# New hand-laid orders, PSUM banks and two VectorE forms in a four-stage transformer kernel

## The chip, the cores and the metric

The program runs on one core of one Trainium2 chip. The metric is the device time of one execution in microseconds (us); lower is better. TensorE is PE in the rows (PEld its weight loads), VectorE DVE, ScalarE ACT, GpSimd POOL, SyncE SP.

## The reference

x has 8 batches of 256 tokens by 128 features, float32. Four residual stages follow each other, each on a layer norm of x:

```
x = x + attn_a(layernorm(x))      # Q, K, V by sigmoid projections; A from |mean Q - mean K|, no softmax; (A @ V) @ Wo + bo
x = x + ffn(layernorm(x))         # w_down(silu(w_gate x) * (w_up x)), 384 hidden, int weights / 127
x = x + attn_b(layernorm(x))      # 16 heads of 64, causal softmax, + biases
x = x + ffn(layernorm(x))         # the same ffn again
```

In attn_a, with t = 1 - mean over features of Q (and of K), delta = t_Q - t_K transposed, f = 0.9 exp(-|delta| / 0.5), and A = f + 0.9 where delta < 0, else -f + 0.9.

## The kernel before

The kernel keeps x in SBUF as 16 tiles of 128 tokens by 128 features, two tiles (256 tokens) to a batch b. The work is cut into small **jobs** with a name and a number; each engine runs its own list of jobs, written out as a string (`ORDER`), so that all 8 batches overlap as a pipeline. Semaphores alone tie the lists together. The letter at the end of a name tells the stage: A is the first attention, F the first ffn, B the softmax attention, P the second ffn.

Jobs of one batch b: lnsA (VectorE makes the statistics at lines 695 to 702, `var` among them; GpSimd makes rstd by a power at line 855 and the normalised xn at line 866, batch 0 has xn on VectorE at line 712), lntA (TensorE transposes xn; ScalarE copies it rounded as xt_hi, line 571, VectorE makes the rest xt_lo, line 768), qkv0 to qkv2 (three f32r matmuls each), mean (means of Q and K; VectorE makes tq, ntk and the 0/1 tile `less`, lines 726 to 732), dist (ScalarE: |delta| and exp), sign (VectorE, `signed`, line 787), stdp (GpSimd), sv, vwo, aout (TensorE; VectorE adds to x, line 743). The ffn: lnsF, lntF, gF0 to gF2 (gate and up matmuls; ScalarE tanh; two VectorE instructions, lines 779 and 780, make the hidden tile), dbF (TensorE, line 430; VectorE adds to x, line 747). The softmax attention: lnsB, lntB (rt_hi, rt_lo), v0 to v3, and for each of the 64 head pairs m: qk.m (six f32r matmuls; VectorE adds the bias, line 824), scores.m (eight short f32 matmuls, two banks s0 and s1), mask.m (VectorE, lines 797 and 799: minus the masked score and its maximum), exp.m (ScalarE), inverse.m (VectorE), norm.m (GpSimd, line 908), transposes.m (TensorE, banks t0 and t1; evacuated by ScalarE and VectorE), and for two pairs together sum.m (line 536). out0 and out1 multiply by Wo and VectorE adds to x (line 754); the last batch has part of them done ahead as pre0, pre1. The second ffn is lnsP, lntP, gP, dbP, and SyncE stores a batch when dbP has been added.

Four more kinds: w0 to w5 split the big weights into wqkv_hi (ScalarE) and wqkv_lo (GpSimd, line 888); bv copies a bias out on VectorE (line 757); bo is a matmul for the output bias (line 442), computed once; hot is filler for TensorE, four transposes of the identity whose result nobody reads.

Matmuls of qkv, g, v and qk have f32r operands; all others have f32 operands, and for each the profile shows two matmuls where the program has one (transposes one). TensorE writes into eight PSUM banks. `BANKS` gives for each job the bank of its n-th instance, one digit each. A bank is taken again only when its reader has released it: `take` waits for that. Rings of buffers limit the head pairs: three for qk, two for neg_s, four for prob.

```
ORDER = {"PE": "lntA.0 hot.0 hot.1 qkv1.0 ...", "ACT": ..., "DVE": ..., "POOL": ...}
def take(job, n):
    if turns[job, n] > 1:
        pe.wait_ge(g_free[bank_of(job, n)], turns[job, n] - 1)
```

In the rows below, L350 to L352 are the f32r matmuls of qkv, v and qk, L368 transposes of lnt, L410 and L411 the ffn's gate and up, L430 db, L449 to L451 the filler, L457 pre, L464 out, L536 sum.

Of the kernel before, what the change touches and what calls it, by code (L numbers as in the profile page):

```python
# [21 lines left out]
P = 128  # L22
# [31 lines left out]
        sum.3 transposes.4 transposes.5 qk.9 aout.2 v2.0 v2.1 scores.8 scores.9 transposes.6 transposes.7 sum.5 qk.10 lntF.2
        v1.1 v3.1 qk.11 gF0.2 scores.10 transposes.8 scores.11 transposes.9 sum.7 lntA.3 gF2.2 gF1.2 qk.12 qk.13 out0.0 qkv0.3
        qkv2.3 dbF.2 scores.12 scores.13 sum.9 transposes.10 transposes.11 qk.14 qk.15 qkv1.3 out1.0 lntB.2 mean.3 transposes.12
        scores.14 sum.11 scores.15 transposes.13 qk.16 lntP.0 vwo.3 qk.17 aout.3 gP0.0 v1.2 v2.2 gP2.0 sum.13 transposes.14
        transposes.15 scores.16 scores.17 v3.2 lntF.3 qk.18 v0.2 qk.19 gF2.3 gF1.3 gF0.3 sum.15 scores.18 transposes.16
        scores.19 transposes.17 gP1.0 out0.1 dbF.3 lntA.4 qk.20 qk.21 sum.17 scores.20 scores.21 transposes.18 transposes.19
        qkv1.4 lntB.3 out1.1 qkv2.4 qkv0.4 qk.22 qk.23 mean.4 scores.22 scores.23 sum.19 transposes.20 transposes.21 qk.24  # L60
        lntP.1 dbP.0 gP0.1 vwo.4 v0.3 qk.25 aout.4 gP2.1 scores.24 scores.25 sum.21 transposes.22 transposes.23 lntF.4 qk.26
        qk.27 v2.3 v1.3 gF0.4 sum.23 scores.26 scores.27 transposes.24 transposes.25 gF2.4 qk.28 gF1.4 lntA.5 qk.29 out0.2 dbF.4
        sum.25 scores.28 transposes.26 transposes.27 scores.29 qkv1.5 gP1.1 out1.2 qkv0.5 qk.30 qk.31 lntB.4 v3.3 mean.5 qkv2.5
        transposes.28 scores.30 scores.31 transposes.29 sum.27 v0.4 dbP.1 lntP.2 vwo.5 qk.32 qk.33 aout.5 gP2.2 scores.32 sum.29
        transposes.30 transposes.31 scores.33 qk.34 lntF.5 v1.4 qk.35 gP0.2 v2.4 gF0.5 transposes.32 scores.34 scores.35 sum.31
        transposes.33 qk.36 gF1.5 lntA.6 gF2.5 out0.3 qk.37 qk.38 dbF.5 qkv1.6 qkv0.6 scores.36 scores.37 transposes.34
# [884 lines left out]
```

## Time and profile before

| | |
|---|---|
| median of 3 runs | 340.31 us (340.23 to 340.88) |
| the profiled execution: its own time | 340.77 us |
| its span, first to last instruction | 338.7 us |
| TensorE busy | 319.7 us (94%) |
| VectorE / ScalarE / GpSimd busy | 269.0 / 231.5 / 198.5 us |
| DMA | 5.83 MB; nearly all in the first 20 us |

The time of an execution is its span and about 2 us around it. A share of busy time is a mean over stages. Matmuls are pipelined, so two of them overlap in the rows and the distance from start to start tells their cost better than their length. An engine's instructions run in the order of its list, so one that is late holds all behind it.

### The profile page before, as it was taken

How to read it: one execution, taken by the hardware profiler on the slowest of the kernel's cores; microseconds unless marked ns; L12 is line 12 of the kernel's file. 1: busy time of each engine (PE TensorE's matmuls, PEld its weight loads, DVE VectorE, ACT ScalarE, POOL GpSimd, SP SyncE). 2: the span in 40 equal slices, each digit the busy share in tenths (PEclk: the TensorE clock that was granted, in tenths of full speed). 3: DMA queues.
4: the chain of work that ended last, by engine and by line, in shares of the span. 5: the costliest groups of instructions: out<-in, count | busy, mean ns of one | idle time of the engine just before them, and what ended most of it. 6: DMA issues, size and time to landing. Idle time of an engine off the chain costs nothing. (4 is left out here: it accounts for less than half of the span.)

```text
span 338.7 us, 9997 instructions
## 1 busy us (share of the span) xinstructions
PE 319.7 (94%) x3264; PEld 278.0 (82%) x3264; DVE 269.0 (79%) x1092; ACT 231.5 (68%) x784; POOL 198.5 (59%) x265
## 2 busy tenths in 40 slices
PE   2888999999999998999999999999999999999995
PEld 2767788889888977889988888889988878888875
DVE  4468799988987889878979879878787897967645
ACT  2643678876688858576887757777868738787811
POOL 4585456778745657947566197742757186355600
PEclk9999999999999999999999999999999999999999
DMA  7900000000000000000000000000000000000001
GB/s 194 296 0 3 1 2 4 2 1 3 2 2 2 2 2 3 15 3 3 2 16 4 2 2 1 18 2 0 4 17 0 3 3 17 3 0 3 3 15 33
DMA packets 6418, 5.83 MB, mean 17 GB/s; under 512 B 864, under 2 KB 5856, under 8 KB 6368
## 3 DMA queue, kind: packets, MB, share of 16 engines
q1 hardware_dynamic: 6080, 4.99, 5.0%
...
HBM read 4.15 MB, written 1.05 MB: 15 GB/s over the span
## 5 line engine op out<-in xcount | busy, mean ns | idle before, releaser
L908 POOL TENSOR_TENSOR prob<-prob,row_inv 128x256 f32<-128x256 f32 (+1 forms) x128 | 102.6, 828 | 87.7 <-DVE row_inv L814 87.7
L640 ACT ACTIVATE prob<-neg_s,neg_max 128x128 f32<-128x128 f32 x128 | 50.7, 396 | 24.5 <-DVE neg_max L799 23.6
L642 ACT ACTIVATE prob<-neg_s,neg_max 128x256 f32<-128x256 f32 x128 | 63.7, 498 | 0.0
L799 DVE CUSTOM_DVE_ANT_0 neg_s<-bank,mask 128x256 f32<-128x256 f32 x128 | 53.6, 419 | 0.0
L536 PE MATMUL bank<-prob_t,v 128*64 128x256 f32 (+1 forms) x512 | 48.5, 332 | 0.9 <-DVE ntk L727 0.7
L824 DVE TENSOR_TENSOR qk<-bank,bqk 128x512 f32<-128x512 f32 x64 | 42.6, 682 | 3.6 <-PE bank L352 3.6
L536 PEld LDWEIGHTS bank<-prob_t,v 128*64 128x64 f32 x512 | 32.9, 136 | 15.4 <-issue 4.9
L797 DVE CUSTOM_DVE_ANT_0 neg_s<-bank,mask 128x128 f32<-128x128 f32 x128 | 36.5, 285 | 10.5 <-PE bank L501 9.6
L650 ACT ACTIVATE prob_t<-bank 128x384 f32<-128x384 f32 x64 | 29.6, 482 | 14.7 <-PE bank L513 14.4
L501 PE MATMUL bank<-qk 64*128 64x256 f32 x256 | 39.0, 377 | 0.0
L350 PE MATMUL bank<-rt_hi,wqkv_hi 128*128 128x256 f32 x128 | 38.8, 303 | 0.2 <-DVE neg_max L799 0.2
L807 DVE COPY prob_t<-bank 128x384 f32<-128x384 f32 x64 | 33.6, 549 | 3.8 <-PE bank L513 3.8
L513 PEld LDWEIGHTS bank<-ident,prob 64*128 64x128 f32 x768 | 29.7, 139 | 7.5 <-issue 4.1
L352 PE MATMUL bank<-rt_lo,wqkv_hi 128*128 128x256 f32 x128 | 35.8, 279 | 0.0
L351 PE MATMUL bank<-rt_hi,wqkv_lo 128*128 128x256 f32 x128 | 35.7, 279 | 0.0
L513 PE MATMUL bank<-ident,prob 64*128 64x64 f32 x768 | 32.6, 225 | 1.5 <-issue 1.4
L498 PE MATMUL bank<-qk 64*128 64x128 f32 x256 | 28.9, 299 | 0.8 <-DVE qk L824 0.8
L464 PE MATMUL bank<-wo,zt 128*128 128x128 f32 x232 | 28.6, 276 | 0.4 <-DVE neg_max L799 0.4
L659 ACT ACTIVATE zt<-bank 128x512 f32<-128x512 f32 x32 | 18.9, 590 | 14.6 <-PE bank L536 14.5
L464 PEld LDWEIGHTS bank<-wo,zt 128*128 128x128 f32 x232 | 27.1, 192 | 0.6 <-issue 0.6
L498 PEld LDWEIGHTS bank<-qk 64*128 64x128 f32 x256 | 21.8, 186 | 6.3 <-issue 2.8
L350 PEld LDWEIGHTS bank<-rt_hi,wqkv_hi 128*128 128x128 f32 x128 | 24.1, 188 | 3.4 <-issue 1.0
...
## 6 DMA issues: line engine op xcount, KB each, us to landing
...
```

The source lines that it names most:

```text
L350: nc.tensor.matmul(out, w_hi_ap, r_hi_ap, start=True, stop=False)
L464: last = nc.tensor.matmul(out[:, 0:D], zt[:, b % 2, u, j * P:(j + 1) * P], wo[:, u, :], start=(u == 0), stop=(u == U - 1))
L498: nc.tensor.matmul(home(f"s{e}", m)[0][:, 0:P], qk[half, r, 0, 0:P], qk[half, r, 1, 0:P], start=True, stop=True)
L501: nc.tensor.matmul(S[:, P:SC], qk[half, r, 0, P:N], qk[half, r, 1, :], start=True, stop=True).then_inc(done, 1)
L513: last = nc.tensor.transpose(out[:, at:at + A], prob[half, m % 4, e, j * P:(j + 1) * P], ident[half, half])
L536: last = nc.tensor.matmul(out[half, t + k * P:t + N], v[:, b % 2, k, h * A:(h + 1) * A], prob_t[:, i % 4, e, cols], start=(k == 0), stop=( ...
L640: nc.scalar.activation(prob[:, r, e, 0:P], neg_s[:, m % 2, e, 0:P], ACT.Exp, bias=neg_max[:, q, 2 * e:2 * e + 1], scale=-1.0, accum_out=ro ...
L642: nc.scalar.activation(prob[:, r, e, P:SC], neg_s[:, m % 2, e, P:SC], ACT.Exp, bias=neg_max[:, q, 2 * e + 1:2 * e + 2], scale=-1.0, accum_ ...
L797: nc.vector.tensor_tensor_reduce(out=neg_s[:, m % 2, e, 0:P], in0=S[:, 0:P], in1=mask[:, P:N], scale=-SCORE_SCALE, scalar=3e38, op0=ALU.ad ...
L799: nc.vector.tensor_tensor_reduce(out=neg_s[:, m % 2, e, P:SC], in0=S[:, P:SC], in1=mask[:], scale=-SCORE_SCALE, scalar=3e38, op0=ALU.add, ...
L824: nc.vector.tensor_tensor(qk[:, m % 3, :, :], W[:].rearrange("p (w s) -> p w s", s=N), bqk[:, u, :].unsqueeze(2).to_broadcast([P, 2, N]), ...
L908: nc.gpsimd.tensor_tensor(pr, pr, inv, ALU.mult).then_inc(p_norm, 1)
```

## The change

All four lists of `ORDER` and all of `BANKS` are written anew. Each job occurs as often as before, but the fillers: 12 instead of 14. The tiles hid_hi, hid_lo and dnt, their semaphores and the branches that used them (jobs hh, hl and dn, which no list contained) are removed. Two VectorE instructions get another form: the variance plus eps, and the compare `less`, which now compares with a tile of zeros (the left half of `mask`) instead of with the constant 0; mean.0 waits for GpSimd's memsets.

```diff
     "PE": """
-        lntA.0 hot.0 hot.1 qkv1.0 qkv0.0 qkv2.0 mean.0 hot.2 lntA.1 hot.3 vwo.0 hot.4 qkv2.1 aout.0 hot.5 qkv1.1 hot.6 hot.7
...
+        lntA.0 hot.0 qkv1.0 qkv0.0 qkv2.0 mean.0 lntA.1 vwo.0 hot.1 hot.2 hot.3 qkv1.1 aout.0 qkv0.1 qkv2.1 hot.4 hot.5 mean.1
+        lntF.0 hot.6 hot.7 gF1.0 gF0.0 gF2.0 bo.0 lntA.2 dbF.0 qkv1.2 qkv0.2 vwo.1 qkv2.2 aout.1 lntB.0 hot.8 qk.0 qk.1 v1.0
...
 BANKS = {
-    "lntA": "61052653",
-    "qkv0": "06524416",
+    "lntA": "77171570",
+    "qkv1": "16736051",
...
-        gate_t, hid, dnt = ({k: sb(f"{n}_{k}", [P, w, N]) for k in "FP"} for n, w in (("gate_t", FC), ("hid", FC), ("dnt", 1)))
-        hid_hi, hid_lo = ({k: sb(f"{n}_{k}", [P, FC, N], F32R) for k in "FP"} for n in ("hid_hi", "hid_lo"))
+        gate_t, hid = ({k: sb(f"{n}_{k}", [P, FC, N]) for k in "FP"} for n in ("gate_t", "hid"))
...
-                    nc.vector.tensor_scalar(var[c][:], mv[c][:, :, 1], EPS, None, ALU.add).then_inc(var_s[k], 1)
+                    nc.vector.scalar_tensor_tensor(var[c][:], mv[c][:, :, 1], EPS, mv[c][:, :, 1], ALU.add, ALU.max).then_inc(var_s[k], 1)
...
+                    if b == 0:
+                        dve.wait_ge(consts_in, 4)
...
-                        last = nc.vector.tensor_scalar(less[:, j, :], tq[:, b % 2, :], ntk[:, b % 2, j:j + 1], 0.0, ALU.add, ALU.is_lt)
+                        last = nc.vector.scalar_tensor_tensor(less[:, j, :].rearrange("p (k s) -> p k s", s=P), tq[:, b % 2, :].rearrange("p (k s) -> p k s", s=P),
+                                                              ntk[:, b % 2, j:j + 1], mask[:, 0:P].unsqueeze(1).to_broadcast([P, T, P]), ALU.add, ALU.is_lt)
```

Three places of the new lists, by instruction. The first is VectorE's list near the front, from the normalised tile of batch 0's layer norm F to its first hidden piece. Before:

```order
L712 TENSOR_SCALAR xn_F<-x,mv_F,rstd_F 128x128 x2
L695 BN_STATS stats_A<-x 128x6 x2
L700 BN_AGGR mv_A<-stats_A 128x2 x2
L702 TENSOR_SCALAR var_A<-mv_A 128x2
L768 TENSOR_TENSOR xt_lo_F<-bank,xt_hi_F 128x256
L779 SCALAR_TENSOR_TENSOR hid_F<-gate_t_F,bank 128x256
L780 TENSOR_TENSOR hid_F<-hid_F,bank 128x256
```

And in the change:

```order
L673 TENSOR_SCALAR xn_F<-x,mv_F,rstd_F 128x128 x2
L721 COPY bv_all<-bv 128x1024
L732 TENSOR_TENSOR xt_lo_F<-bank,xt_hi_F 128x256
L689 TENSOR_SCALAR tq<-bank 128x256
L690 TENSOR_SCALAR ntk<-bank 128x2
L695 SCALAR_TENSOR_TENSOR less<-tq,ntk,mask 128x256 x2
L740 SCALAR_TENSOR_TENSOR hid_F<-gate_t_F,bank 128x256
L741 TENSOR_TENSOR hid_F<-hid_F,bank 128x256
```

The statistics of the next batch's norm A are gone from here (they stand ahead of aout.0), and mean.1 with its two compares has moved from behind the three hidden pieces to ahead of them; sign.1 follows the hidden pieces and stands ahead of the add of dbF.0.

The second is TensorE's list from mean.1 (before) or the last gate job (change) of the same stretch on. Before:

```order
L381 MATMUL bank<-t_qkv,mean_w 128x256
L383 MATMUL bank<-mean_w,t_qkv 128x1 x2
L430 MATMUL bank<-wd,hid_F 128x128 x6
L449 MATMUL bank<-ident 128x128 x2
L450 MATMUL bank<-ident 128x128
L451 MATMUL bank<-ident 128x128
L442 MATMUL bank<-wo,bv_all 128x128 x8
L368 MATMUL bank<-ident,xn_A 128x128 x2
L399 MATMUL bank<-vwo,stdp 128x128 x4
L368 MATMUL bank<-ident,xn_B 128x128 x2
```

And in the change:

```order
L402 MATMUL bank<-xt_lo_F,wu 128x256
L418 MATMUL bank<-wo,bv_all 128x128 x8
L359 MATMUL bank<-ident,xn_A 128x128 x2
L411 MATMUL bank<-wd,hid_F 128x128 x6
L341 MATMUL bank<-xt_hi_A,wa_hi 128x256
L342 MATMUL bank<-xt_hi_A,wa_lo 128x256
L343 MATMUL bank<-xt_lo_A,wa_hi 128x256
```

bo.0 and lntA.2 now stand ahead of dbF.0, and behind it come qkv1.2, qkv0.2, vwo.1, qkv2.2, aout.1 and then lntB.0.

The third is the end of TensorE's list, from the last part of the last batch's output on. Before:

```order
L457 MATMUL bank<-wo,zt 128x128 x6
L464 MATMUL bank<-wo,zt 128x128 x4
L410 MATMUL bank<-xt_hi_P,wg 128x256
L411 MATMUL bank<-xt_lo_P,wg 128x256
L410 MATMUL bank<-xt_hi_P,wu 128x256
L411 MATMUL bank<-xt_lo_P,wu 128x256
L449 MATMUL bank<-ident 128x128 x2
L450 MATMUL bank<-ident 128x128
L451 MATMUL bank<-ident 128x128
```

And in the change:

```order
L359 MATMUL bank<-ident,xn_P 128x128 x2
L433 MATMUL bank<-wo,zt 128x128 x6
L440 MATMUL bank<-wo,zt 128x128 x4
L411 MATMUL bank<-wd,hid_P 128x128 x6
L401 MATMUL bank<-xt_hi_P,wg 128x256
L402 MATMUL bank<-xt_lo_P,wg 128x256
L401 MATMUL bank<-xt_hi_P,wu 128x256
L402 MATMUL bank<-xt_lo_P,wu 128x256
```

dbP.5 and gP1.6, which stood well ahead of the last out jobs, now stand behind them, followed by gP2.6 and one filler instead of three. The add of dbP.5 stands on VectorE next to those of dbP.6 and dbP.7.

## Rows read from the trace of the kernel before

**Rows 1.** The page, part 1: busy us (share of the span) xinstructions of each engine.
```profile
PE 319.7 (94%) x3264; PEld 278.0 (82%) x3264; DVE 269.0 (79%) x1092; ACT 231.5 (68%) x784; POOL 198.5 (59%) x265
```

**Rows 2.** Busy time by stretch: us, length, PE PEld DVE ACT POOL (x), PEclk, DMA, GB/s.
```profile
6.60:34.00 27.40, 23.21 (x154) 20.44 (x155) 18.16 (x61) 13.58 (x30) 17.68 (x22) 1.00 0.35 109
34.00:325.30 291.30, 287.31 (x3043) 249.69 (x3042) 241.21 (x1001) 214.16 (x747) 177.15 (x231) 1.00 0.02 5
```

**Rows 3.** The timeline of the front: start us, us, engine, instruction [idle before <-releaser].
```profile
7.89 0.42 DVE L768 TENSOR_TENSOR xt_lo_A<-bank,xt_hi_A 128x256 fp32r<-128x256 f32 x1
8.64 0.56 PE L350 MATMUL bank<-xt_hi_A,wa_hi 128*128 128x256 f32 x1
...
20.99 0.38 ACT L571 ACTIVATE xt_hi_F<-bank 128x256 fp32r<-128x256 f32 x1 [3.14 <-PE bank L368]
21.17 1.05 DVE L702 TENSOR_SCALAR var_A<-mv_A 128x2 f32<-128x2 f32 x1
22.14 0.41 DVE L768 TENSOR_TENSOR xt_lo_F<-bank,xt_hi_F 128x256 fp32r<-128x256 f32 x1
22.65 0.35 PE L410 MATMUL bank<-xt_hi_F,wg 128*128 128x256 f32 x1 [0.57 <-issue]
23.81 0.42 DVE L779 SCALAR_TENSOR_TENSOR hid_F<-gate_t_F,bank 128x256 f32<-128x256 f32 x1 [1.26 <-ACT gate_t_F L594]
26.36 1.58 PE L430 MATMUL bank<-wd,hid_F 128*128 128x128 f32 x12 [0.57 <-DVE hid_F L780]
26.70 1.45 DVE L732 TENSOR_SCALAR less<-tq,ntk 128x256 f32<-128x256 f32 x2
28.66 0.41 DVE L747 SCALAR_TENSOR_TENSOR x<-bank,x 128x256 f32<-128x256 f32 x1
29.00 0.68 DVE L787 SCALAR_TENSOR_TENSOR signed<-less,expd 128x512 f32<-128x512 f32 x1
...
33.51 0.38 PE L350 MATMUL bank<-rt_hi,wqkv_hi 128*128 128x256 f32 x1
```

**Rows 4.** The timeline of TensorE near the end: dbP.5, lntP.6; gP1.6, transposes.
```profile
314.73 1.60 PE L430 MATMUL bank<-wd,hid_P 128*128 128x128 f32 x12
316.17 0.38 PE L368 MATMUL bank<-ident,xn_P 128*128 128x128 f32 x2
...
319.33 0.38 PE L410 MATMUL bank<-xt_hi_P,wg 128*128 128x256 f32 x1
320.00 0.96 PE L513 MATMUL bank<-ident,prob 64*128 64x64 f32 x24
```

**Rows 5.** One variance group (ns min/median/max), and timeline rows of VectorE, GpSimd and TensorE.
```profile
L702 DVE TENSOR_SCALAR var_A<-mv_A x8: 169/169/1053, 4.8 to 163.7; 128x2 f32<-128x2 f32 x8
...
6.64 0.73 POOL L873 TENSOR_TENSOR xb<-x,boa 128x256 f32<-128x256 f32 x1
6.70 0.68 DVE L717 SCALAR_TENSOR_TENSOR ga_scale<-ga_rs,ga 128x3 f32<-128x3 f32 x1 [0.23 <-POOL ga_rs L858]
...
59.13 0.83 DVE L787 SCALAR_TENSOR_TENSOR signed<-less,expd 128x512 f32<-128x512 f32 x1
...
121.48 0.38 PE L498 MATMUL bank<-qk 64*128 64x128 f32 x2 [0.79 <-DVE qk L824]
```

**Rows 6.** The timeline of TensorE: first matmuls of qk.42, qk.43, qk.44, qk.45.
```profile
220.36 0.28 PE L350 MATMUL bank<-rt_hi,wqkv_hi 128*128 128x256 f32 x1
221.06 0.28 PE L350 MATMUL bank<-rt_hi,wqkv_hi 128*128 128x256 f32 x1
...
231.23 0.37 PE L350 MATMUL bank<-rt_hi,wqkv_hi 128*128 128x256 f32 x1
232.02 0.28 PE L350 MATMUL bank<-rt_hi,wqkv_hi 128*128 128x256 f32 x1
```

**Rows 7.** The page, part 5: the two mask instructions, busy us, mean ns | idle before.
```profile
L799 DVE CUSTOM_DVE_ANT_0 neg_s<-bank,mask 128x256 f32<-128x256 f32 x128 | 53.6, 419 | 0.0
L797 DVE CUSTOM_DVE_ANT_0 neg_s<-bank,mask 128x128 f32<-128x128 f32 x128 | 36.5, 285 | 10.5 <-PE bank L501 9.6
```

More of the change, by code:

```diff
@@ L54 @@
[L54 to L66, printed above, removed]
@@ L67 @@
-        transposes.35 sum.33 gP1.2 mean.6 out1.3 qk.39 qkv2.6 lntB.5 sum.35 scores.38 scores.39 transposes.36 transposes.37
-        vwo.6 v3.4 qk.40 qk.41 v0.5 aout.6 lntP.3 dbP.2 scores.40 scores.41 transposes.38 transposes.39 sum.37 gP2.3 qk.42 qk.43
-        lntF.6 gP0.3 v2.5 v1.5 gF0.6 sum.39 transposes.40 scores.42 scores.43 transposes.41 gF2.6 lntA.7 gF1.6 out0.4 qk.44
-        qk.45 gP1.3 dbF.6 qkv0.7 qkv1.7 sum.41 scores.44 scores.45 transposes.42 transposes.43 qk.46 mean.7 qkv2.7 lntB.6 qk.47
@@ new lines @@
+        qkv0.3 qkv1.3 scores.12 scores.13 transposes.9 out1.0 transposes.10 transposes.11 vwo.3 qk.15 mean.3 lntB.2 scores.14
+        scores.15 sum.9 sum.11 transposes.12 transposes.13 lntP.0 v2.2 qk.16 v1.2 gP0.0 gP2.0 qk.17 aout.3 sum.13 transposes.14
+        scores.16 scores.17 transposes.15 v3.2 gP1.0 lntF.3 qk.18 qk.19 qk.20 gF1.3 gF0.3 v0.2 sum.15 transposes.16 scores.18
+        scores.19 transposes.17 gF2.3 qk.21 lntA.4 out0.1 dbF.3 sum.17 scores.20 scores.21 transposes.18 transposes.19 out1.1
@@ new lines @@
+        qkv2.4 qkv1.4 qkv0.4 qk.22 qk.23 mean.4 lntB.3 scores.22 scores.23 sum.19 lntP.1 dbP.0 qk.24 v0.3 qk.25 qk.26 vwo.4
+        transposes.20 transposes.21 aout.4 gP2.1 gP0.1 sum.21 scores.24 scores.25 v2.3 lntF.4 qk.27 v1.3 transposes.22
+        transposes.23 scores.26 scores.27 transposes.24 sum.23 qk.28 lntA.5 gF1.4 gF0.4 out0.2 gF2.4 transposes.25 qk.29 gP1.1
+        qkv1.5 qkv0.5 dbF.4 sum.25 scores.28 scores.29 transposes.26 transposes.27 qk.30 mean.5 qk.31 v3.3 out1.2 lntA.6 qkv2.5
@@ new lines @@
+        lntB.4 scores.30 scores.31 sum.27 vwo.5 qk.32 v1.4 qk.33 lntP.2 dbP.1 scores.32 scores.33 transposes.28 transposes.29
+        aout.5 v2.4 gP2.2 qk.34 qk.35 transposes.30 transposes.31 sum.29 lntF.5 v0.4 qkv1.6 gP0.2 gF0.5 gF1.5 gF2.5 sum.31
+        scores.34 scores.35 transposes.32 transposes.33 qk.36 qk.37 qkv0.6 dbF.5 scores.36 scores.37 gP1.2 out1.3 qk.38 qk.39
+        qkv2.6 mean.6 lntB.5 out0.3 transposes.34 transposes.35 scores.38 scores.39 transposes.36 sum.33 sum.35 v0.5 vwo.6 qk.40
```

260 lines of the change are left out of this document (111 added, 149 removed).

## The prediction

> **What bounds the kernel now.** I read the page first, then the busy time of each engine by stretch, then the timeline at both ends, and last the rows of the instructions that are rewritten. The page shows TensorE busy 94% of a span of 338.7 us; VectorE has 79%, GpSimd 59% [rows 1]. By stretch [rows 2]: before 34 us TensorE is busy 23.21 of 27.40 us, and part of that is filler (the hot jobs). Between 34.00 and 325.30 us it is busy 287.31 of 291.30: 3.99 us idle. So nothing that makes another engine faster can be worth more than those 4 us in the middle. The rest must come from work moved into the ends, where TensorE waits for a chain through all engines, or from cheaper junctions between TensorE's own jobs.
>
> At the front the chain is batch 0: attention output, layer norm F, hidden layer, layer norm B, first qk. The reader is to see two places where it is late [rows 3]. At 21.17 VectorE takes 1.05 us over the variance of lnsA.2, and only then starts xt_lo_F at 22.14, though ScalarE had finished xt_hi_F at 20.99 + 0.38 = 21.37; TensorE's first gate matmul comes at 22.65. And the dbF.0 matmuls end at 26.36 + 1.58 = 27.94, but VectorE is in the two compares (26.70, 1.45 us) and the copy of bv, and starts the add to x at 28.66. At the other end a chain with little choice runs from out1.7 to the last store.
>
> **The change part by part.** Sums are against the profiled execution's span.
>
> *Front.* lnsA.2 now stands ahead of aout.0 on VectorE, where it waits anyway, and the copy of bv stands in the gap before xt_hi_F is ready: xt_lo_F can start at 21.37, the gates at 21.9, 0.77 us earlier. Then mean.1 is put ahead of the hidden layer on VectorE (tq, ntk, two compares, some 1.4 us). They end near 23.2; the first gate is ready at 21.9 + 1.16 (22.65 to 23.81 before) = 23.05. So the hidden layer starts at 23.2 and not 23.81, and TensorE does bo.0 in that gap. dbF.0 starts 0.65 us earlier and ends at 27.3, and nothing stands between it and the add: x at 27.35 instead of 28.66, 1.3 us earlier. sign.1, which ran at 29.00 between x and lnsB.0, is now ahead of dbF.0: 0.6 us more. One filler less stands before qkv1.0, which can start when xt_lo_A ends at 7.89 + 0.42 = 8.31 and not at 8.64: 0.3 us. And lntB.0 no longer stands on VectorE behind two jobs that came in late (xt_lo_A, bo_all): 0.3 us. So the first qk matmul comes near 31.0 instead of 33.51: 2.5 us. In addition qkv2.2 is now done before it: three matmuls at 0.12 us, 0.4 us. **Front: -2.9 us.** The jobs put between dbF.0 and lntB.0 (two qkv, vwo.1, qkv2.2, aout.1, 2.6 us together) fit in the 3 us that the chain takes there. GpSimd is moved too: two of its wqkv_lo pieces went from ahead of the first rstd_F to behind rstd_B; they are done by about 32, when v1.0 asks for them. Bounds: -3.3 if every gap closes; -1.2 if the compares wait for GpSimd (below).
>
> *Tail.* dbP.5 (314.73 to 316.17, 1.44 us) and gP1.6 (319.33 to 320.00, 0.67 us) stood ahead of out0.7 and now stand behind out1.7 [rows 4], where three fillers ran while the last batch's x was normalised; they take the place of two fillers: 2.1 us gained. Against it: on VectorE the hidden pieces gP2.6 and gP0.6, some 0.8 us each, both stand behind the last batch's xt_lo now; the first gate is ready 1.2 us after it, so 0.4 us is lost. One more store is issued at the end, ahead of the last one, and is hidden. **Tail: -1.7 us**, bounds -2.1 and -0.9.
>
> *The middle's waits.* 3.99 us are there; the largest kind is seen at 121.48, where TensorE waited 0.79 us for a qk that VectorE brought late behind a variance [rows 5]. In the new lists the distance from scores to their transposes grows (some 12 us of other TensorE jobs at the median against 9, an estimate from the jobs' lengths in this trace), and a PSUM bank is taken again after less than 1 us of other jobs some 14 times against 25. I take half of the waits as gone: **-2.0 us**, bounds -4.0 and +4.0, since a new order brings waits of its own.
>
> *Junctions.* The same six qk matmuls take 0.70 us from start to start behind another f32r job (220.36 to 221.06) and 0.79 behind an f32 job (231.23 to 232.02) [rows 6]. Such changes of kind fall from 74 to 63. At 0.09 each that is 1.0 us, but f32 jobs in succession, which rise from 190 to 199, have longer starts too. **-0.4 us**, bounds -1.0 and 0.
>
> *Forms.* The variance takes 169 ns at the least and up to 1053 [rows 5]. The new form reads mv twice; whether that frees it from GpSimd, two rows tell differently. signed, with two SBUF operands, ran at 59.13 beside the end of a norm and took 0.83 us, where its eight instances have 0.68 at the least: 0.15 lost. But ga_scale at 6.70, three elements, took 0.68 us and ended with GpSimd's xb at 6.64 + 0.73 = 7.37. The compare becomes such an instruction over 256 elements, about 0.4 us by signed's 0.83 for 512, 0.1 dearer than now; 16 of them make 1.6 us of VectorE beside TensorE's work. **0**, bounds -1.0 and +1.7. The Trainium skill (SBUF — State Buffer, Who interferes with whom) says that a VectorE instruction with two SBUF inputs contends with a GpSimd instruction that reads SBUF, under an exclusive lock in which the second blocks fully. By that rule the sum would be rival (a)'s; ga_scale agrees with it, signed at 59.13 does not. The wait that is added, mean.0 for the four memsets, is over long before: the identity made from one of them is used in the first transpose. The removed buffers and branches ran nothing: 0.
>
> Sum: 338.7 - 2.9 - 1.7 - 2.0 - 0.4 = 331.7 us of span. The profiled execution took 340.77, 2.07 around its span, and the median of the three runs is 0.46 below it. So 331.7 + 2.07 - 0.46 = **333.3 us**.
>
> **The rivals.** (a) *The new forms wait in full.* If a VectorE instruction with two SBUF operands stands until GpSimd's is over, as at ga_scale, the compares of mean.1, now ahead of the hidden layer, wait there as they did at 26.70 (1.45 us for two): the front gives 1.2 us instead of 2.9, and the other seven compares add 0.1 us each: 333.3 + 1.7 + 0.8 = 335.8. For it: ga_scale; against it: signed. (b) *The wider distances take nearly all waits away*: 2 us more, and 1 us of small lateness in starts: 330.3. (c) *The gain is given back*: TensorE comes to the same scores 3 us sooner, VectorE (241.21 us busy of 291.30 in the middle) does not follow, and waits there grow by 5 to 6 us: 339 to 340. (d) *Slower: bunched scores.* Of scores behind scores there are now 32 instead of 22, with three triples (52 to 54, 56 to 58, 59 to 61) that want six of the eight banks. VectorE needs 2 x (285 + 419) ns = 1.41 us to empty one pair [rows 7], TensorE fills one in about 0.7. A bunch that finds no free bank costs the difference, 0.7 us. It decides from ten such waits on, which eat the 7.0 us of the forecast; with twelve the time is 333.3 + 8.4 = 341.7. Against it: the jobs between bunches are longer than before, and the banks are chosen anew.
>
> **How the numbers follow.** Forecast 0.55 (331 to 335), (a) 0.14, (b) 0.14, (c) 0.09, (d) 0.08. A measurement of this kernel tells 0.2%, 0.7 us, from no change. Below 339.6 lie the forecast, (a), (b) and half of (c): 0.88 faster; 0.04 same; 0.08 slower. The range 329.5 to 338.5 takes in the forecast, (a) and (b) with their bounds and leaves out (c) and (d), 0.17.
>
> **What would show it.** Right: the first qk matmul near 31 us; out0.7 starting near 318; under 2.5 us of TensorE idle between these two; variances that stay below 0.5 us. Wrong: a variance or compare that still ends with a GpSimd instruction (a); TensorE waiting on banks that the masks release in the triples (d); TensorE idle more than 4 us in the middle (c).

## The result and the profile after

| | before | changed |
|---|---|---|
| median | 340.43 us (340.23 to 340.88, 4 runs) | 334.87 us (333.27 to 335.18, 4 runs) |
| a second set, other chip time | 340.31 us (339.92 to 340.66, 15 runs) | 334.35 us (333.62 to 335.38, 4 runs) |
| profiled execution, span | 340.77 us, 338.7 us | 333.27 us, 331.2 us |
| TensorE / VectorE / ScalarE / GpSimd busy | 319.7 / 269.0 / 231.5 / 198.5 us | 313.8 / 267.9 / 230.8 / 201.2 us |

The ratio is 0.9829, with a 95% interval from 0.9803 to 0.9855; in the second set it is 0.9828 (0.9809 to 0.9847). The change is faster by some 5.8 us. The forecast was 333.3 us, 1.6 below the first median and 1.1 below the second. Two things are new. The executions of the changed kernel lie over 1.9 us, those of before over 0.65; and the profiled one is the fastest of its four, so its trace shows a better front than most executions have. One of the runs below is about that.

The page's first part and the stretches of the changed kernel, which answer to [rows 1, 2] (columns as in rows 2):

```profile
PE 313.8 (95%) x3256; PEld 274.8 (83%) x3256; DVE 267.9 (81%) x1092; ACT 230.8 (70%) x784; POOL 201.2 (61%) x265
```

```profile
6.60:34.00 27.40, 23.31 (x163) 20.45 (x164) 19.71 (x65) 14.23 (x31) 18.41 (x22) 1.00 0.34 108
34.00:317.40 283.40, 280.39 (x3013) 244.99 (x3012) 237.70 (x994) 212.52 (x744) 179.30 (x232) 1.00 0.02 4
317.40:331.20 13.80, 10.13 (x84) 9.32 (x82) 8.12 (x25) 2.58 (x7) 0.72 (x1) 1.00 0.11 30
```

TensorE's idle time in the middle is 283.40 - 280.39 = 3.01 us, against 3.99. That is only 1 us less. The rest of the gain is not idle time, and the stretches between the same jobs show where it lies. From the first qk matmul to out0.7 the kernel before needs 291.81 us (33.51 to 325.32), with TensorE busy 287.82; the changed one needs 285.23 us (32.19 to 317.42), busy 282.22:

```profile
32.19:317.42 285.23, 282.22 (x3025) 246.78 (x3026) 239.44 (x1000) 212.83 (x745) 181.01 (x233) 1.00 0.02 4
```

The front gave 33.51 - 32.19 = 1.3 us, the middle 6.6, and the tail took 0.4 (13.38 to 13.80 us from out0.7 to the end): 7.5 us of span. The middle is the part that repeats: five traces with the changed middle untouched, the new compare in it (this one, a_again, a_wlo, a_fill, a_prefill), have 285.22 to 285.35 us, the two of the old middle (before, b_tail) 291.81 and 291.83. The front, which answers to [rows 3] (timeline; start us, us, engine, instruction, idle before and its releaser):

```profile
20.51 0.38 ACT L547 ACTIVATE xt_hi_F<-bank 128x256 fp32r<-128x256 f32 x1 [1.15 <-PE bank L359]
20.92 0.42 DVE L732 TENSOR_TENSOR xt_lo_F<-bank,xt_hi_F 128x256 fp32r<-128x256 f32 x1 [0.35 <-ACT xt_hi_F L547]
21.24 1.93 POOL L827 TENSOR_SCALAR xn_A<-x,mv_A,rstd_A 128x128 f32<-128x128 f32 x2
21.45 0.36 PE L401 MATMUL bank<-xt_hi_F,wg 128*128 128x256 f32 x1
21.78 0.89 DVE L695 SCALAR_TENSOR_TENSOR less<-tq,ntk,mask 128x256 f32<-128x256 f32 x2
22.60 0.42 DVE L740 SCALAR_TENSOR_TENSOR hid_F<-gate_t_F,bank 128x256 f32<-128x256 f32 x1
...
25.31 1.57 PE L411 MATMUL bank<-wd,hid_F 128*128 128x128 f32 x12 [0.25 <-DVE hid_F L741]
26.93 0.42 DVE L711 SCALAR_TENSOR_TENSOR x<-bank,x 128x256 f32<-128x256 f32 x1 [0.25 <-PE bank L411]
27.95 1.27 POOL L849 TENSOR_TENSOR wqkv_lo<-wqkv,wqkv_hi 128x512 fp32r<-128x512 f32 x1
28.19 1.05 DVE L663 SCALAR_TENSOR_TENSOR var_B<-mv_B 128x2 f32<-128x2 f32 x1
29.32 0.72 POOL L816 TENSOR_TENSOR rstd_B<-var_B,minus_half 128x2 f32<-128x2 f32 x1
30.73 0.44 PE L359 MATMUL bank<-ident,xn_B 128*128 128x128 f32 x2 [0.95 <-DVE xn_B L673]
32.19 0.36 PE L341 MATMUL bank<-rt_hi,wqkv_hi 128*128 128x256 f32 x1 [0.41 <-DVE rt_lo L732]
```

Up to the add of dbF.0 the front is better than forecast: the gates start at 21.45 (21.9 was forecast), x is added at 26.93 (27.35). Then it loses what it had gained. The variance of lnsB.0 starts at 28.19 and lasts until 29.24, as GpSimd's wqkv_lo ends at 27.95 + 1.27 = 29.22. In the kernel before, the same instruction at 30.39 took 0.17 us, because that piece of wqkv_lo was not there. This is the full wait of rival (a), at a place that the forecast had not looked at.

The variance and the compare by groups, which answer to [rows 5] (ns min/median/max):

```profile
L663 DVE SCALAR_TENSOR_TENSOR var_A<-mv_A x8: 160/162/995, 5.0 to 179.4; 128x2 f32<-128x2 f32 x8
L663 DVE SCALAR_TENSOR_TENSOR var_B<-mv_B x8: 160/163/1051, 28.2 to 270.9; 128x2 f32<-128x2 f32 x8
L663 DVE SCALAR_TENSOR_TENSOR var_P<-mv_P x7: 160/161/1019, 85.6 to 310.7; 128x2 f32<-128x2 f32 x7
...
L695 DVE SCALAR_TENSOR_TENSOR less<-tq,ntk,mask x16: 473/547/1257, 12.6 to 232.4; 128x256 f32<-128x256 f32 x16
```

The variance still goes up to 1.05 us. Nine of its 32 instances take over 0.25 us, against 15 before. The compare's least time is 0.47 us; in the kernel before the compare took 0.33 at the least.

### The profile page after: what moved, and what is told of

Same layout as the page of the kernel before. It is cut to its first block, busy times and chain, and to the rows that moved or that the text cites. A ratio compares the mean times of both kernels' runs of the same rounds, so it can differ in the third digit from the quotient of the medians.

```text
span 331.2 us, 9981 instructions
## 1 busy us (share of the span) xinstructions
PE 313.8 (95%) x3256; PEld 274.8 (83%) x3256; DVE 267.9 (81%) x1092; ACT 230.8 (70%) x784; POOL 201.2 (61%) x265
## 3 DMA queue, kind: packets, MB, share of 16 engines
HBM read 4.15 MB, written 1.05 MB: 16 GB/s over the span
## 4 chain that ended last, share of the span: by engine, by line
PE 76%; DVE 8%; issue 6%; POOL 5%; ACT 3%; DMA 1%; DVEq 0%; ACTq 0%; POOLq 0%
PE bank L512 11%; PE bank L477 7%; PE bank L440 7%; PE bank L341 7%; PE bank L489 7%; PE bank L342 6%; PE bank L343 6%; PE bank L411 5%; PE bank L474 5%; PE bank L401 3%; PE bank L402 3%; PE bank L359 2%; PE bank L390 2%; POOL wqkv_lo L849 1%; DMA x<-x_in 1%
## 5 line engine op out<-in xcount | busy, mean ns | idle before, releaser
L862 POOL TENSOR_TENSOR prob<-prob,row_inv 128x256 f32<-128x256 f32 (+1 forms) x128 | 103.7, 836 | 62.4 <-DVE row_inv L775 62.3
L601 ACT ACTIVATE prob<-neg_s,neg_max 128x128 f32<-128x128 f32 x128 | 50.5, 395 | 12.3 <-DVE neg_max L760 11.8
L512 PE MATMUL bank<-prob_t,v 128*64 128x256 f32 (+1 forms) x512 | 47.1, 331 | 0.1
L758 DVE CUSTOM_DVE_ANT_0 neg_s<-bank,mask 128x128 f32<-128x128 f32 x128 | 36.5, 285 | 12.5 <-PE bank L477 10.5
L512 PEld LDWEIGHTS bank<-prob_t,v 128*64 128x64 f32 x512 | 32.1, 136 | 13.6 <-issue 3.2
L341 PE MATMUL bank<-rt_hi,wqkv_hi 128*128 128x256 f32 x128 | 38.0, 297 | 0.4 <-DVE rt_lo L732 0.4
L474 PE MATMUL bank<-qk 64*128 64x128 f32 x256 | 28.0, 294 | 1.2 <-issue 0.7
```

Source lines behind the costliest of these rows:

```text
L341: nc.tensor.matmul(out, w_hi_ap, r_hi_ap, start=True, stop=False)
L474: nc.tensor.matmul(home(f"s{e}", m)[0][:, 0:P], qk[half, r, 0, 0:P], qk[half, r, 1, 0:P], start=True, stop=True)
L512: last = nc.tensor.matmul(out[half, t + k * P:t + N], v[:, b % 2, k, h * A:(h + 1) * A], prob_t[:, i % 4, e, cols], start=(k == 0), stop=( ...
L601: nc.scalar.activation(prob[:, r, e, 0:P], neg_s[:, m % 2, e, 0:P], ACT.Exp, bias=neg_max[:, q, 2 * e:2 * e + 1], scale=-1.0, accum_out=ro ...
L862: nc.gpsimd.tensor_tensor(pr, pr, inv, ALU.mult).then_inc(p_norm, 1)
```

## The experiments

A name that starts with a is the changed kernel with an edit, one with b the kernel before with an edit. "Middle" is the time from the first qk matmul to out0.7 in the run's trace.

### Does the execution or the kernel differ?

a_again is the changed kernel without an edit.

> The changed kernel itself, unaltered, for a second trace and more times. Its first four executions took 333.27 (the profiled one), 334.66, 335.08 and 335.18 us, spans 331.2 to 333.1. Theory: a few short VectorE instructions wait for a GpSimd instruction in one execution and not in the next, about 1 us each, so the executions spread over some 2 us: median 334 to 335.3, and the new trace, if it is a longer one, differs from the first in two or three such places, in the front above all. Rival: the spread is in the load of x and the weights at the start; then the first transpose starts 1 us or more later than 6.82 us and the rest of the trace is the same.

334.35 us median (333.62 to 335.38), ratio 0.9828. Its trace starts lntA.0 at 6.70, 0.12 earlier than the first trace, but the first qk matmul comes at 33.56, 1.4 later. From there on the two are alike: middle 285.35 and 285.23 us, tail 13.82 and 13.80. So both theories named the wrong cause: no VectorE instruction waits longer, and the load is not late. The fillers show what differs (timeline of TensorE, the second instruction of a filler). First trace:

```profile
7.70 0.42 PE L426 MATMUL bank<-ident 128*128 128x128 f32 x1
13.86 0.27 PE L426 MATMUL bank<-ident 128*128 128x128 f32 x1
```

a_again:

```profile
7.57 0.42 PE L426 MATMUL bank<-ident 128*128 128x128 f32 x1
14.41 0.42 PE L426 MATMUL bank<-ident 128*128 128x128 f32 x1
15.64 0.42 PE L426 MATMUL bank<-ident 128*128 128x128 f32 x1
16.80 0.27 PE L426 MATMUL bank<-ident 128*128 128x128 f32 x1
```

TensorE is on the lower of its two clock levels (1.2 and 2.4 GHz; the next transpose starts 0.21 us later, 0.11 on the upper level) until 10.5 us in one execution and until 16.8 in the other. The granted clock in the rows of the stretches says 1.00 in both. That it is the clock is read from the instructions alone: f32 transposes and f32r matmuls double their distance together. Followed job by job, TensorE in a_again is 0.12 us ahead of the first trace up to 10.98 us and 1.36 behind at 15.30, and 1.37 at the first qk. So the late rise costs this front 1.5 us. That is most of the spread's 1.9 us; the executions without a trace can't be put down to it for certain.

### The forms

a_oldforms takes both old forms back (the diffs of this part have the operands shortened).

```diff
-  scalar_tensor_tensor(var, mv, EPS, mv, ALU.add, ALU.max)
+  tensor_scalar(var, mv, EPS, None, ALU.add)
-  scalar_tensor_tensor(less, tq, ntk, zeros, ALU.add, ALU.is_lt)
+  tensor_scalar(less, tq, ntk, 0.0, ALU.add, ALU.is_lt)
```

> The changed kernel with the variance and the compare in their old forms (one SBUF tile operand and constants). Theory: both forms wait alike until a GpSimd instruction with two tile inputs (norm, wqkv_lo) is over: 9 of 32 variances of the changed kernel took 0.3 to 1.05 us, as 16 of 32 did before; so the form itself is worth nothing: within 0.7 us of the changed kernel (334.1 to 335.6), the compare 341 to 360 ns at the least instead of 473. Rival (the new form waits in full where the old one does not): 1.7 us or more faster than the changed kernel. Other rival (the new form frees the instruction from GpSimd and that is what was gained): 337 us or more.

333.53 us (332.83 to 334.57), ratio 0.9804 (0.9787 to 0.9821): by the medians 0.8 to 1.3 us faster than the changed kernel, although its trace has the clock rise latest of all, at 18 us. The intervals of the two ratios overlap, so the whole time alone does not settle it; the middle does, 284.34 us, 0.9 less. Between the expectations: the forms are not free, they cost.

b_newforms puts them alone into the kernel before.

> The kernel before with the two new forms alone, its orders and banks untouched. Theory: the same time as before within 0.7 us (339.7 to 341.1); about half of the 32 variances still take over 0.25 us. Rival (forms free VectorE from GpSimd): 339.0 or less, and no variance over 0.3 us. Rival (they wait more): 341.5 or more.

341.66 us (341.25 to 342.14), ratio 1.0041 (1.0028 to 1.0053): 1.4 us slower than before. Middle 292.96 us against 291.81, 1.15 more. The variance waits as it did (14 of 32 over 0.25 us, against 15); the compare takes 0.47 us at the least. It stands before masks and qk on VectorE, and TensorE's idle time from 34 us to out0.7 is 292.30 - 287.43 = 4.87 us, against 3.99. The compare's group and that stretch:

```profile
L734 DVE SCALAR_TENSOR_TENSOR less<-tq,ntk,mask x16: 471/484/1300, 12.7 to 243.0; 128x256 f32<-128x256 f32 x16
```

```profile
34.00:326.30 292.30, 287.43 (x3042) 249.73 (x3041) 242.63 (x1000) 214.05 (x747) 177.73 (x231) 1.00 0.02 5
```

a_oldless takes back the compare alone.

```diff
-  scalar_tensor_tensor(less, tq, ntk, zeros, ALU.add, ALU.is_lt)
+  tensor_scalar(less, tq, ntk, 0.0, ALU.add, ALU.is_lt)
```

> The changed kernel with only the compare in its old form; the variance keeps the new one. The two old forms together took 0.8 to 1.3 us less than the changed kernel, and the new ones added 1.3 us to the kernel before. Theory: the cost is the compare's, 473 against 341 ns at the least, 16 times, on VectorE where qk and masks stand behind it; the variance is the same in both forms (161 against 169 ns): so this one is within 0.4 us of the run with both old forms, 333.2 to 333.9. Rival: the variance's second read makes it wait more often; then this one stays at 334.3 to 335.

332.23 us (332.01 to 333.74), ratio 0.9764 (0.9742 to 0.9786). Faster than expected. Its middle is 284.41 us, the same as with both old forms, so the whole cost of the forms in the middle, 0.9 us, is the compare's (four traces with its old form have 284.28 to 284.41 us, the five named above 285.22 to 285.35):

```profile
L695 DVE TENSOR_SCALAR less<-tq,ntk x16: 343/384/1126, 13.2 to 232.0; 128x256 f32<-128x256 f32 x16
```

The rest of the 2.1 to 2.6 us to the changed kernel is not in the middle. In the trace the clock rose at 12.4 us (see below); how many of the other executions had an early rise can't be seen. Both forms of the variance wait until a norm or a wqkv_lo on GpSimd is over: with the old one in the kernel before at 21.17 [rows 3], beside wqkv_lo; with the new one var_B above. Beside GpSimd's normalisation (xn, one tile and two scalars) both ran at nearly their own speed (the variance 0.16 to 0.27 us in 24 cases), as the compares at 21.78 beside xn_A at 21.24 above. The Trainium skill (SBUF — State Buffer, Who interferes with whom) has a rule for each form: a VectorE instruction with two SBUF inputs contends with a GpSimd instruction that reads SBUF, and so do copy, cast and tensor_scalar where they enter a mode with two ports. The traces agree for norm and wqkv_lo on GpSimd; for xn, which reads SBUF too, they don't.

`signed` waits in full as well. The prediction took its 0.83 us at 59.13 [rows 5] as a sign against that, because the wait seemed to cost 0.15 only. The norm beside it says otherwise; two other pairs stand behind it (the kernel before, twice, then b_front):

```profile
58.37 1.04 POOL L908 TENSOR_TENSOR prob<-prob,row_inv 128x512 f32<-128x512 f32 x1
```

```profile
198.37 0.72 POOL L855 TENSOR_TENSOR rstd_A<-var_A,minus_half 128x2 f32<-128x2 f32 x1
198.41 0.17 DVE L702 TENSOR_SCALAR var_B<-mv_B 128x2 f32<-128x2 f32 x1
```

```profile
25.32 0.41 POOL L883 TENSOR_SCALAR sv<-t_qkv 128x256 f32<-128x256 f32 x1
25.37 0.90 DVE L787 SCALAR_TENSOR_TENSOR signed<-less,expd 128x512 f32<-128x512 f32 x1
```

The norm ends at 59.41, `signed` at 59.96, 0.55 us later. In the 14 traces `signed` starts beside a running norm or wqkv_lo 22 times, with 0.24 to 1.19 us of it left, and ends 0.54 or 0.55 us after it every time. So the wait is full, and some 0.13 us of its 0.68 pass during it. The other two pairs show that the number of tiles is not the rule: rstd has two (of two elements) and the variance runs free beside it; sv has one, and `signed` ends 0.54 us after it. What sets xn and rstd apart from norm, wqkv_lo and sv stays open.

### The tail

b_tail is the kernel before with dbP.5 and gP1.6 moved behind out1.7 as in the change, and their readers with them; lntP.6 stays ahead of sum.59, where the change has it behind sum.63.

```diff
-  dbP.5 lntP.6 sum.59 sum.61 gP1.6 ... out0.7 out1.7 gP2.6 hot.10 hot.11 hot.12 lntP.7
+  lntP.6 sum.59 sum.61 ... out0.7 out1.7 dbP.5 gP1.6 gP2.6 hot.10 lntP.7
```

> The kernel before with the change's tail alone: dbP.5 and gP1.6 behind out1.7 on TensorE, their readers moved on VectorE and ScalarE likewise, two fillers less there. Theory: 1.7 us less than before (338.7; bounds -2.1 and -0.9), out0.7 starting 1.9 to 2.1 us earlier than at 325.3 and 0 to 0.4 us more from there to the end. Rival: the jobs were hidden anyway or make the last batch late, so the time stays within 0.5 us of before.

340.66 us (340.17 to 341.22, 11 runs), ratio 1.0012 (1.0004 to 1.0021). The rival holds: nothing gained, even 0.4 lost. The timeline of TensorE shows why (in the kernel before, lntP.6 at 316.17 and the transposes at 320.00 have no idle time before them [rows 4]):

```profile
314.40 0.60 PE L501 MATMUL bank<-qk 64*128 64x256 f32 x4
316.05 0.44 PE L368 MATMUL bank<-ident,xn_P 128*128 128x128 f32 x2 [1.05 <-POOL xn_P L866]
316.42 3.19 PE L536 MATMUL bank<-prob_t,v 128*64 128x256 f32 x32
319.54 0.59 PE L513 MATMUL bank<-ident,prob 64*128 64x64 f32 x12
320.54 0.59 PE L513 MATMUL bank<-ident,prob 64*128 64x64 f32 x12 [0.42 <-POOL prob L908]
```

With dbP.5 gone, lntP.6 waits 1.05 us for GpSimd's normalised x; with gP1.6 gone, the last transposes wait 0.42 us for GpSimd's norm. The two jobs had covered these waits: in the kernel before they cost next to nothing where they stood.

a_tailback goes the other way: in the changed kernel dbP.5 goes back ahead of transposes.60, and its add on VectorE with it.

```diff
-  ... sum.57 transposes.60 ... out0.7 out1.7 dbP.5 gP1.6 gP2.6
+  ... sum.57 dbP.5 transposes.60 ... out0.7 out1.7 gP1.6 gP2.6
```

> The changed kernel with dbP.5 taken back from behind out1.7 to ahead of transposes.60, where TensorE waits 0.43 us for GpSimd. In the kernel before, the same kind of move forward gave nothing, as lntP.6 and transposes.63 then waited 1.05 and 0.42 us for GpSimd, which dbP.5 and gP1.6 had covered. Theory: in the new order what stands there is not waiting for GpSimd but for 0.43 us, so dbP.5 (1.44 us) costs 1.0 us there: 0.7 to 1.2 us slower than the changed kernel, out0.7 later by that. Rival: it is covered there as well, and the time is the same within 0.3 us: then the tail's gain does not exist in the changed kernel either.

335.48 us (334.32 to 336.37), ratio 0.9848 (0.9826 to 0.9871): by the medians 0.6 to 1.1 us slower than the changed kernel, with intervals that overlap. The middle settles it, 286.40 us, 1.17 longer; the tail is as long as in the changed kernel (13.79). The recorded reason was a wait of 0.43 us for GpSimd ahead of transposes.60, which dbP.5 would fill. The wait is there in the changed kernel, and 1.51 us of dbP.5 less 0.43 are 1.08 of the 1.17 us; but by the changed kernel's trace it is a wait for VectorE's copy out of a bank:

```profile
308.29 0.40 PE L489 MATMUL bank<-ident,prob 64*128 64x64 f32 x6 [0.43 <-DVE prob_t L768]
```

Behind out1.7, where dbP.5 is missing, the trace of a_tailback shows a hole:

```profile
322.55 0.44 PE L359 MATMUL bank<-ident,xn_F 128*128 128x128 f32 x2 [1.53 <-DVE xn_F L673]
```

So in the changed kernel the step for dbP.5 is worth about 1 us, and in the kernel before nothing (gP1.6 alone was not tried there). What differs, by the rows, is the place of lntP.6: the new order has it behind sum.63, where it waits for nobody, with transposes.62 and 63 ahead of it. No run moved lntP.6 alone.

```profile
315.81 0.44 PE L359 MATMUL bank<-ident,xn_P 128*128 128x128 f32 x2
```

### The front

b_front has the change's lists up to lntB.0 (on GpSimd up to w4.0), with nine fillers there, and the order of before from the first qk on.

```diff
-  lntA.0 hot.0 hot.1 qkv1.0 ... dbF.0 hot.9 bo.0 lntA.2 aout.1 lntB.0 qkv0.2 qkv1.2 qk.0
+  lntA.0 hot.0 qkv1.0 ... bo.0 lntA.2 dbF.0 qkv1.2 qkv0.2 vwo.1 qkv2.2 aout.1 lntB.0 hot.8 qk.0
```

> The kernel before with the changed front alone: every engine's list up to lntB.0 (GpSimd's up to the last of its early wqkv_lo pieces) is the change's, with its banks, its nine fillers instead of ten, and qkv2.2 read by ScalarE early; from the first qk on all is as before, old forms throughout. Theory: the front gives 1.3 us at the first qk matmul where the clock rises early (32.2 instead of 33.5) and 0 where it rises late, plus 0.4 us for qkv2.2: out0.7 0.4 to 1.8 us earlier than at 325.3, time 338.6 to 340.0. Rival (the full term of the prediction, 2.9 us): 337.5. Rival: the gain is lost in the waits of the old middle: 340.2 or more.

340.75 us (339.25 to 341.78, 12 runs), ratio 1.0004 (0.999 to 1.0018): no gain in the median. In its trace, whose clock rose at 12 us, the first qk matmul is at 32.23 and the gain is there, 1.3 us. Out0.7 comes only 0.75 us earlier than in the kernel before (324.57 against 325.32), since the middle is longer than expected, 292.34 us, though qkv2.2 is done ahead: TensorE waits in it for a normalised x of GpSimd, which it did not before:

```profile
PE bank L368 <- POOL xn_F L866: 1.0, 1, 1.0
```

And its twelve executions lie over 2.5 us, where the other variant of the kernel before, b_tail, had eleven over 1.05. The spread came in with the new front. So the median holds the new wait in the middle and, most likely, a late clock in some executions, which have no trace.

a_wlo moves two pieces of wqkv_lo on GpSimd into a gap of 2.8 us in the changed kernel.

```diff
-  lnsA.0 lnsA.1 sv.0 stdp.0 lnsF.0 lnsA.2 w5.0 sv.1 w0.0 stdp.1 w2.0 lnsB.0 w1.0 w4.0 lnsF.1 ...
+  lnsA.0 lnsA.1 sv.0 stdp.0 w2.0 w4.0 lnsF.0 lnsA.2 w5.0 sv.1 w0.0 stdp.1 lnsB.0 w1.0 lnsF.1 ...
```

> The changed kernel with two of GpSimd's wqkv_lo pieces (w2.0, w4.0) moved from around lnsB.0 to ahead of lnsF.0, where GpSimd stood idle for 2.8 us. Theory: in both traces of the changed kernel the variance of lnsB.0 took 1.05 us because wqkv_lo (1.27 us) ran on GpSimd; without it the variance takes 0.16 us and the first qk matmul comes 0.9 us earlier after the end of dbF.0 (5.5 us from the first dbF.0 matmul to the first qk matmul instead of 6.88): 0.9 us less in all. Rival: qk.0 then waits for the pieces themselves or for TensorE's own jobs, and nothing is gained; or the two pieces make the variance of lnsF.0 late, and it is slower.

333.46 us (332.12 to 334.46), ratio 0.9791 (0.9767 to 0.9815), by the medians 0.9 to 1.4 us less than the changed kernel. From the first dbF.0 matmul to the first qk matmul it is 5.99 us (26.45 to 32.44) and not 6.88: 0.9 us, as expected, though not down to 5.5. The variance is free:

```profile
29.32 0.16 DVE L663 SCALAR_TENSOR_TENSOR var_B<-mv_B 128x2 f32<-128x2 f32 x1
```

### The clock

a_fill puts the two fillers of the front back.

```diff
-  lntA.0 hot.0 qkv1.0 qkv0.0 qkv2.0 mean.0 lntA.1 ...
+  lntA.0 hot.0 hot.1 qkv1.0 qkv0.0 qkv2.0 mean.0 hot.2 lntA.1 ...
```

> The changed kernel with the two fillers of the front back in their old places (one more before qkv1.0, one between mean.0 and lntA.1). In the traces so far a filler's second instruction takes 0.42 us until TensorE's clock rises and 0.27 after; the rise comes at 9.7 to 12.3 us in three traces of the old order with 14 fillers, and at 10.4, 16.7 and 17.9 in three of the changed order with 12. Theory: the missing fillers let the clock rise later in most executions, and that makes the 1.4 to 2 us between the first trace and the others of the changed kernel; so with them back the clock has risen by 12.5 us, the first qk matmul comes at 31.8 to 32.6 and the median is 333.0 to 333.8, spread under 1 us. Rival: the time of the rise has nothing to do with the fillers; then it still comes after 16 us in this trace or the next, and the median stays at 334.3 to 335.

333.61 us (333.41, 333.48, 333.61, 333.80 and one at 335.39), ratio 0.9805 (0.9783 to 0.9827). In the trace the clock rises at 10 us. Four executions agree within 0.4 us and one is 1.8 above, and the interval of the ratio overlaps the changed kernel's: the fillers may help, but do not settle it.

a_prefill has six fillers ahead of lntA.0 besides.

```diff
-  lntA.0 hot.0 qkv1.0 qkv0.0 qkv2.0 mean.0 lntA.1 ...
+  hot.0 hot.1 hot.2 hot.3 hot.4 hot.5 lntA.0 hot.6 hot.7 qkv1.0 qkv0.0 qkv2.0 mean.0 hot.8 lntA.1 ...
```

> The changed kernel with eight more fillers in the front: six ahead of lntA.0, where TensorE stands idle from 2 to 6.8 us while batch 0's x is loaded and normalised, one more before qkv1.0 and one behind mean.0. Theory: TensorE's clock has then risen (a filler's second instruction 0.27 instead of 0.42 us) before the first qkv matmul at 8.5 us, in every execution, and the front runs at the upper level throughout: qkv1.0 to mean.0 2.0 us instead of 2.33, the first qk matmul at 31.3 to 32.2, median 332.0 to 333.2, spread under 1 us. Rival: the early fillers do not hold the clock up across the 1 us before lntA.0, so the rise still comes between 10 and 18 us and the median stays at 334.3 to 335; or they end after lntA.0 could start, and each us of that is lost.

335.43 us (335.43 to 335.62), ratio 0.9856 (0.9843 to 0.9868). The theory is wrong in its main point: TensorE works from 1.95 us on with pauses of 0.15 us and still stays on the lower level until 11.8:

```profile
1.95 0.69 PE L425 MATMUL bank<-ident 128*128 128x128 f32 x2 [1.95 <-POOL ident L805]
3.21 0.66 PE L425 MATMUL bank<-ident 128*128 128x128 f32 x2
...
9.04 0.63 PE L359 MATMUL bank<-ident,xn_A 128*128 128x128 f32 x2
...
11.13 0.42 PE L426 MATMUL bank<-ident 128*128 128x128 f32 x1
...
11.93 0.28 PE L343 MATMUL bank<-xt_lo_A,wa_hi 128*128 128x256 f32 x1
```

A filler takes 1.24 us from start to start there, so lntA.0 comes 2.2 us late, and all behind it. What it did do is make the executions alike: 0.2 us between the four.

The clock in all traces:

| kernel | fillers up to the first qk | upper level from | first qk matmul | span |
|---|---|---|---|---|
| before; b_tail; b_newforms | 10 | 12.1; 12.4; 9.9 | 33.51; 33.66; 33.40 | 338.7; 339.1; 339.8 |
| changed; a_again | 9 | 10.5; 16.8 | 32.19; 33.56 | 331.2; 332.7 |
| a_oldforms; a_oldless | 9 | 18.0; 12.4 | 34.14; 32.58 | 332.3; 330.8 |
| a_wlo; a_tailback; b_front | 9 | 15.9; 11.0; 12.1 | 32.44; 32.20; 32.23 | 331.5; 332.4; 338.0 |
| a_fill | 11 | 10.0 | 32.46 | 331.5 |
| a_prefill; a_best | 17 | 11.9; 9.5 | 34.46; 34.02 | 333.4; 332.2 |
| a_last | 13 | 14.5 | 32.91 | 330.9 |

With the fillers of before the rise was never later than 12.4 us (three traces); with one less it came three times in seven after 15. That is a hint, and a_last (below), with more fillers and a rise at 14.5, speaks against it. What decides the rise stays open.

### Two versions from what was found

a_best has the compare's old form, the GpSimd lists of a_wlo and the fillers of a_prefill.

> The changed kernel with three edits together: the compare in its old form, the two wqkv_lo pieces moved ahead of lnsF.0, and the eight fillers of the run beside it. Theory: the gains add, since they lie in different places: 2.1 us (compare, by its own run against the changed kernel's first and second sets of times, 334.6 to 332.2; 0.9 of it in the middle by the trace), 0.9 (pieces), about 1 (clock): 330.5 to 331.8. Rival: part of what the compare's run gained was an early clock, as its trace had, so that the clock's part is counted twice: 331.0 to 332.2. Rival: no sum, the front is then bound by something else: 332.0 or more.

334.18 us (333.12 to 334.30), ratio 0.9811 (0.9795 to 0.9827). The six fillers cost it the 2.2 us at lntA.0 (9.03 us) that they cost a_prefill; against that one it is 1.3 us faster.

a_last has three fillers there instead of six, and none added before qkv1.0.

```diff
-  lntA.0 hot.0 qkv1.0 qkv0.0 qkv2.0 mean.0 lntA.1 ...
+  hot.0 hot.1 hot.2 lntA.0 hot.3 qkv1.0 qkv0.0 qkv2.0 mean.0 hot.4 lntA.1 ...
```

> The changed kernel with the compare in its old form, the two wqkv_lo pieces ahead of lnsF.0, three fillers ahead of lntA.0 instead of six, and one behind mean.0. With six, a filler took 1.24 us from start to start at the lower clock level, they ended at 9.0 us and lntA.0 came 2.2 us late; three end at 1.95 + 3 x 1.24 = 5.7 us, before lntA.0 can start at 6.7. Theory: lntA.0 at 6.7 to 6.9, the clock has risen by 12.5 us, dbF.0 to the first qk matmul 6.0 us or less (6.88 in the changed kernel): the sum of the compare's run (332.2) less 0.9 is 331.3, range 330.6 to 332.0, spread under 1 us, the fastest of all. Rival: the rise still comes after 15 us in some executions; then the median is 332 to 333.5 and the spread 1.5 us or more.

333.18 us (332.45 to 334.04), ratio 0.9798 (0.9778 to 0.9818). lntA.0 is in time (6.55), but the clock rises only at 14.5, as the rival has it, and from dbF.0 to the first qk matmul it is 6.72 us and not 6.0. Where the piece's 0.9 us went, two rows of GpSimd and VectorE show. In a_wlo `signed` of batch 1 starts 0.08 us ahead of wqkv_lo:

```profile
26.62 0.69 DVE L748 SCALAR_TENSOR_TENSOR signed<-less,expd 128x512 f32<-128x512 f32 x1 [0.43 <-issue]
26.70 1.75 POOL L849 TENSOR_TENSOR wqkv_lo<-wqkv,wqkv_hi 128x512 fp32r<-128x512 f32 x1
```

In a_last it comes 0.10 us behind it, and the add of dbF.0 stands behind `signed`:

```profile
26.22 1.27 POOL L848 TENSOR_TENSOR wqkv_lo<-wqkv,wqkv_hi 128x512 fp32r<-128x512 f32 x1
26.32 1.72 DVE L747 SCALAR_TENSOR_TENSOR signed<-less,expd 128x512 f32<-128x512 f32 x1 [0.39 <-issue]
```

The one that starts first runs at its own length (0.69 or 1.27 us), the other waits for it (1.75 or 1.72). The four traces of the new order with the compare's old form all have wqkv_lo first (a_oldforms, a_oldless, a_best, a_last), the six with the new form have `signed` first (changed, a_again, a_wlo, a_tailback, a_fill, a_prefill). So the two edits do not add: the earlier compare loses in the front about what the moved pieces gain there. The fastest by median is a_oldless, 332.23 us, 2.1 to 2.6 us below the changed kernel; the medians of a_last and a_wlo lie within its spread. The median of each of these three is below both kernels of the case; only a_oldless has its interval clear of the changed kernel's (0.9809 to 0.9847).

## Why the prediction was right, step by step

The forecast (333.3; 331 to 335) held, the medians being 334.87 and 334.35, in its upper part. Its terms did not hold one by one.

- **Front, -2.9.** In the profiled execution 1.3 us at the first qk matmul, and qkv2.2 done ahead, 0.4: -1.7. Up to the add of dbF.0 the steps were right and a little too small: 1.73 us (28.66 to 26.93) against 1.3, and 0.3 for the filler. Of the filler's 0.3 us, 0.19 came: from the start of xt_lo_A to qkv1.0 it is 0.75 us before (7.89 to 8.64) and 0.56 in the changed kernel (8.08 to 8.64), whose load happened to be 0.19 late. From the add to the variance the move of sign.1 gave 0.47 us, not 0.6. From the variance to the first qk matmul the 0.3 us for lntB.0 did not come at all: 3.12 us before (30.39 to 33.51) and 3.12 in a_wlo (29.32 to 32.44), where the variance does not wait. And the step "GpSimd is moved too: two of its wqkv_lo pieces" was priced only by when the pieces are done, and not by who stands beside them on VectorE: var_B took 0.9 us more, which a_wlo gave back. Over all executions the term is smaller still, since the clock can rise late, as in a_again's: b_front, with a wait of 1 us new in its middle besides, shows none of it in the median.
- **Tail, -1.7.** The working took the two jobs off the path at full price. b_tail shows what it left out, the question of what is late next. Next were lntP.6 and the last transposes, both waiting for GpSimd, 1.05 and 0.42 us; alone, the move costs 0.4. Within the new order a_tailback gives it 1.0 to 1.2 for dbP.5. The loss of 0.4 behind xt_lo was right: 13.38 to 13.80.
- **The middle's waits, -2.0.** As the prediction drew it, half of 3.99 us idle, the term was too large: the idle time fell by 1.0. But the middle is 6.6 us shorter, and that carries the result. Moved out of it are dbP.5, gP1.6 and qkv2.2, 2.5 us by the rows; 4.1 remain, and that with a compare that cost 0.9. So the opening's reading, that the 4 us of idle time are the store of waits in the middle, failed: 4.1 us went while the idle time fell by 1.0. What else went is, for the most part, lateness inside a busy TensorE: its records touch each other while the starts come late. An estimate by the distance usual between kinds of neighbours, from the trace of before, has this lateness and the waits fall together by 3.8 us, from 7.5 to 3.7; coarser kinds (by tile names alone) give a fall of 2.4 to 3.3, from other levels. The direction is safe, the size is not. The forecast had named a small lateness only in rival (b).
- **Junctions, -0.4.** What is left of the 4.1 us is 0.3 by the first estimate and up to 1.7 by the coarser ones; nothing measured them alone.
- **Forms, 0 (-1.0 to +1.7).** Inside the bounds, on the bad side: +1.4 in the kernel before, 0.9 in the middle of the changed one. "16 of them make 1.6 us of VectorE beside TensorE's work" was the failing sentence: 0.13 us more, 16 times, are 2.1 us of VectorE, and about half of it came through to TensorE. "Variances that stay below 0.5 us" was wrong too.
- **Rivals.** (a) was right on the mechanism: the forms wait in full for GpSimd's norm and wqkv_lo, old and new alike. The row held against it, signed at 59.13, was misread: it shows a full wait too. And (a) priced as new what the old compare did already, 1.45 us for two at 26.70. It was wrong on the place: the compares of mean.1, on which it hung its 1.7 us, ran free beside xn_A (0.89 us for two). (c) and (d) did not come: out0.7 is at 317.42, and in the triples (270.4, 285.6 and 293.4 us) TensorE has no idle time.
- **The sum.** Front and tail were too large by some 1.2 and, alone, by 2; the middle too small by nearly the same. The total was right because errors of both signs met, which is luck.

Taken alone, by their ratios, the front gives +0.1 (its interval holds no change), the tail +0.4 and the forms +1.4; the whole gives -5.8. So what is left for the order and banks of the middle, with what they let the other two do, is about -7.7. The order of before with single edits could not show that; new orders with the old banks were not run. Whether order or banks carry it stays open.
